# The first batch of a fused mixer and mixture-of-experts layer, rewritten as one instruction list per engine

## The chip, the cores and the metric

One core of a Trainium2 chip runs the whole program. The metric is the device time of one execution in microseconds, lower is better.

## The reference, cut to what matters

Sixteen batches of 512 tokens by 128 features go through one layer. First a state-space mixer with 8 heads of 64:

```python
z = x @ Wz; ssm = x @ Win              # ssm: B (64), C (64), dt (8), X (512)
delta = softplus(dt + dt_bias)
h = exp(-delta*exp(A_log)) * h + X_t (x) (delta*B_t);  y_t = h @ C_t     # scan over 512 tokens
y = y + D_param * X                    # the skip term
x = layernorm(x + (y * (silu(z) @ Wzg)) @ Wout)
```

Then a mixture of 12 experts of which 3 are chosen for each of three routers (`dw1`, `dw2`, `dw3`):

```python
h = gelu(sum_e (x @ W1[e].T) * dw1[:, e]);  y = sum_e (h @ W2[e].T) * dw2[:, e] + dw3 @ b2
x = layernorm(x + y)
```

## The kernel before, in words

Batches are numbered 0 to 15. Nearly all weights are held as a rounded part and a rest (`w_hi`, `w_lo`), and so are the operands they meet, so that one product is three matmuls (`mm3`, L223): hi by hi, hi by rest, rest by hi. W1 and W2 are 24 tiles of 128x512, tiles 0 to 11 W1, 12 to 23 W2. Each must be loaded, rounded (`w_hi`, ACT, L411) and its rest taken (`w_lo`, POOL, L415; the first two on DVE). `split_w` does that, `load_w` (L386, SP) the load into a slot that an earlier tile has left.

`program` (L1432) runs the same Python functions once for each engine; each function issues only what `eng` is. `mixer_alone` (L1275) does batch 0's mixer and routing and the front of batch 1's mixer. Then `body` (L1177) runs for b = 1 to 15: the experts of batch b-1 are interleaved with the heads of batch b's mixer. `mixture_alone` ends it.

The mixer of a batch: `mix_x` transposes x on PE; `mix_dt` and `mix_step` make delta, a chain of small POOL operations with one reciprocal on DVE (L527); `mix_bc`, `mix_z`, `mix_X`, `mix_zg` are products; `mix_rates` writes decays and their running products to DRAM, from where SP broadcasts one row for each head (`seg_row`, L684, into `seg_b`, and `start_row`, L688, into `ctd`); `mix_states` makes the chunk states. For each head, ACT scales the scores (`mix_score_step`, L782, `Gh`), DVE adds the skip term (`mix_score_skip`, L791) and scans the decays (`mix_decay`, L802), POOL multiplies the two (L809). For each pair of heads PE then runs `mix_y` (L827, L835) and DVE gates the result (L844); `mix_out` is the output product (L853). `seg_b` has two buffers: the row of head h+2 is loaded when scan h is over.

Routing: normalisation (`route_stats`, `route_scale`, L899), a transpose, logits (L943), `route_weights` on DVE (L963 to L987), and `route_rows`: the weights are transposed on PE (L1001), written to DRAM and read back as broadcast rows (`row_b`, L1017). An expert's input is that row times x (`expert_row`, DVE, L1032), rounded on ACT (L1053), its rest on POOL (L1056), then 12 matmuls (`expert_in`, L229 to L231).

What sets the order around the change is this one shared list of calls: every engine takes them in turn. `mix_bank` (L234) gives the mixer's products two PSUM banks in rotation; `keep_busy` (L1270) issues dummy matmuls. POOL takes the rests of tiles 2 to 15 before the first normalised rows are written:

```python
def first_weights_ready(eng):
    if eng in (PE, DVE, AC):
        eng.wait_ge(sems["w_lo0"], rests(N1 - 1))      # N1 = 16
```

since `x1` lies in a slot of the ring that the first 16 tiles pass through. The last two tiles are split among the first experts.

## Time and profile before

| what | value |
|---|---|
| median of 3 runs | 1603.38 us (1601.7 to 1604.11) |
| the profiled execution, its own time | 1602.08 us |
| its span, first to last instruction | 1600.0 us |
| mean granted TensorE clock | 0.993 |
| PE busy | 1564.8 us (98%) |
| first expert matmul of the program | 98.36 us after the span's start |

The span is what the trace covers; the execution's own time is 2.08 us longer. Starts in the trace count from the span's start.

### The profile page before, as it was taken

The page shows a single profiled execution, that of the slowest core. Times are in us where ns is not written, and L with a number is a line of the kernel's source. Part 1 is how long each engine was busy: PE and PEld are TensorE (multiplying, and loading weights), DVE is VectorE, ACT ScalarE, POOL GpSimd, SP SyncE. Part 2 cuts the span into 40 slices and gives each one's busy share as a digit, 9 for nine tenths or more (in the row PEclk, how much of TensorE's full clock was granted, in tenths as well). Part 3 has the DMA queues.
Part 4 walks back from the last instruction along what each step waited for, and adds up shares of the span by engine and source line. Part 5 has one row for each costly group of instructions (what it writes and reads, how often), then busy time and mean ns, then how long its engine had stood idle before and what let it go on. Part 6 is the DMA issues. An engine that isn't in the chain of part 4 may idle for free.

```text
span 1600.0 us, 25283 instructions
## 1 busy us (share of the span) xinstructions
PE 1564.8 (98%) x8632; PEld 1254.4 (78%) x8632; DVE 1105.2 (69%) x3105; ACT 593.8 (37%) x1356; POOL 655.0 (41%) x758
## 2 busy tenths in 40 slices
PE   7789999999999999999999999999999999999997
PEld 6667878787787877878788787878778787887876
DVE  6566677776767776687776767777676776757744
ACT  5542442524334252442425334242442415334130
POOL 5763351715436162351715435162351615335040
PEclk9899999999999999999999999999999999999999
DMA  4441230402214031230402214041230403213020
GB/s 143 136 127 40 64 97 28 133 14 86 76 42 117 28 112 42 65 96 28 133 14 91 77 42 118 22 117 36 64 96 28 133 14 100 68 49 112 21 66 7
DMA packets 81871, 115.30 MB, mean 72 GB/s; under 512 B 10176, under 2 KB 37328, under 8 KB 81744
## 3 DMA queue, kind: packets, MB, share of 16 engines
q1 hardware_dynamic: 81744, 113.71, 24.2%
q8 instruction: 68, 1.11, 0.3%
q14 instruction: 59, 0.48, 0.1%
HBM read 108.55 MB, written 5.13 MB: 71 GB/s over the span
## 4 chain that ended last, share of the span: by engine, by line
PE 94%; POOL 2%; DVE 1%; issue 1%; ACT 1%; DMA 1%; POOLq 0%; SPq 0%; DVEq 0%; ACTq 0%
PE exp_bank L229 23%; PE exp_bank L231 22%; PE exp_bank L230 22%; PE mix_bank L827 4%; PE mix_bank L229 4%; PE mix_bank L853 3%; PE mix_bank L231 3%; PE mix_bank L230 3%; PE mix_bank L835 3%; PE mix_bank L753 1%; PE turn_bank L1106 1%; PE mix_bank L701 1%; PE mix_bank L943 1%; PE mix_bank L502 1%; POOL w_lo L415 1%
## 5 line engine op out<-in xcount | busy, mean ns | idle before, releaser
L1056 POOL TENSOR_TENSOR sp_lo<-fbuf,sp_hi 128x512 fp32r<-128x512 f32 (+2 forms) x208 | 250.0, 1206 | 263.7 <-ACT sp_hi L1053 139.4
L229 PE MATMUL exp_bank<-w_hi,sp_hi 128*128 128x512 f32 x768 | 309.7, 403 | 2.0 <-POOL sp_lo L1099 2.0
L229 PE MATMUL exp_bank<-sp_hi,w_hi 128*128 128x512 f32 x768 | 307.8, 401 | 1.4 <-POOL sp_lo L1056 1.4
L231 PE MATMUL exp_bank<-w_hi,sp_lo 128*128 128x512 f32 x768 | 303.4, 395 | 0.0
L230 PE MATMUL exp_bank<-w_lo,sp_hi 128*128 128x512 f32 x768 | 303.1, 395 | 0.0
L231 PE MATMUL exp_bank<-sp_hi,w_lo 128*128 128x512 f32 x768 | 302.6, 394 | 0.0
L230 PE MATMUL exp_bank<-sp_lo,w_hi 128*128 128x512 f32 x768 | 301.1, 392 | 0.0
L1053 ACT CAST sp_hi<-fbuf 128x512 fp32r<-128x512 f32 (+2 forms) x208 | 122.0, 588 | 309.4 <-DVE fbuf L1032 266.6
L1145 DVE SCALAR_TENSOR_TENSOR acc<-exp_bank,dw,acc 128x128 f32<-128x128 f32 x384 | 132.3, 344 | 141.4 <-PE exp_bank L231 140.8
L229 PEld LDWEIGHTS exp_bank<-sp_hi,w_hi 128*128 128x128 f32 x768 | 144.1, 188 | 45.3 <-issue 13.7
L809 POOL TENSOR_TENSOR Wt<-Wt,Gh 128x512 f32<-128x512 f32 x128 | 176.3, 1378 | 6.2 <-DVE Wt L802 6.0
L535 POOL TENSOR_TENSOR delta<-delta,bias_b 128x32 f32<-128x32 f32 x16 | 4.0, 252 | 423.3 <-ACT delta L512 423.3
L229 PEld LDWEIGHTS exp_bank<-w_hi,sp_hi 128*128 128x128 f32 x768 | 144.3, 188 | 35.3 <-issue 2.0
L231 PEld LDWEIGHTS exp_bank<-w_hi,sp_lo 128*128 128x128 f32 x768 | 144.0, 188 | 35.1
L230 PEld LDWEIGHTS exp_bank<-w_lo,sp_hi 128*128 128x128 f32 x768 | 144.4, 188 | 31.6
L231 PEld LDWEIGHTS exp_bank<-sp_hi,w_lo 128*128 128x128 f32 x768 | 144.3, 188 | 30.9
L230 PEld LDWEIGHTS exp_bank<-sp_lo,w_hi 128*128 128x128 f32 x768 | 144.4, 188 | 30.0
L782 ACT ACTIVATE Gh<-Gm,delta 128x128 f32<-128x128 f32 x512 | 163.5, 390 | 9.8 <-POOL Wt L809 9.8
L802 DVE TENSOR_TENSOR_SCAN Wt<-seg_b,unit_bank 128x512 f32<-128x512 f32 x128 | 154.3, 1206 | 2.0 <-DMA seg_b<-dA_rows 2.0
L1032 DVE TENSOR_TENSOR fbuf<-turn_bank,row_b 128x512 f32<-128x512 f32 x192 | 129.5, 678 | 24.0 <-DMA row_b<-dw_rows 21.5
L1145 DVE SCALAR_TENSOR_TENSOR acc_odd<-exp_bank,dw,acc_odd 128x128 f32<-128x128 f32 x320 | 109.5, 342 | 0.0
L1099 POOL TENSOR_TENSOR sp_lo<-fbuf,sp_hi 128x512 fp32r<-128x512 f32 x32 | 42.6, 1330 | 134.4 <-DVE sp_hi L1093 134.4
(201 smaller groups left out, 2274.4 us busy)
## 6 DMA issues: line engine op xcount, KB each, us to landing
row_b<-dw_rows SPq DMA_DIRECT2D x192, 256.0 KB, 3.4
seg_b<-dA_rows SPq DMA_DIRECT2D x128, 256.0 KB, 3.6
ctd<-cum_rows SPq DMA_DIRECT2D x128, 96.0 KB, 3.3
x_in<-in_x SPq DMA_DIRECT2D x16, 256.0 KB, 2.8
result<-acc SPq DMA_DIRECT2D x16, 256.0 KB, 2.3
fbuf<-in_W1T SPq DMA_DIRECT2D x12, 256.0 KB, 3.1
fbuf<-in_W2T SPq DMA_DIRECT2D x4, 256.0 KB, 2.9
Gh<-in_W2T SPq DMA_DIRECT2D x4, 256.0 KB, 3.8
```

What stands on the lines that cost most here:

```text
L229: nc.tensor.matmul(ps, s_hi, m_hi, start=start and j == 0, stop=False)
L230: nc.tensor.matmul(ps, s_hi, m_lo, start=False, stop=False)
L231: last = nc.tensor.matmul(ps, s_lo, m_hi, start=False, stop=stop and j == n - 1)
L782: last = AC.activation(G[:, c, :], Gm[:, c, :], ACT.Copy, scale=delta[:, c, h:h + 1])
L802: sig("scan", DVE.tensor_tensor_scan(W, seg_b[h % 2][:, :], unit[:, :], 0.0, ALU.mult, ALU.add))
L809: sig("W", PO.tensor_tensor(W, W, Gh[h % 2][:, :, :].rearrange("p c t -> p (c t)"), ALU.mult))
L827: PE.matmul(ps[j * HD:(j + 1) * HD, tok(c)], Xd[:, c, h * HD:(h + 1) * HD], Wt[:, q % 2, at:at + P], start=(c == 0), stop=False)
L835: last = PE.matmul(ps[j * HD:(j + 1) * HD, tok(c)], S[n, c - 1, q * HD:(q + 1) * HD], ctd[n, q % 2, (c - 1) * P:c * P], start=False, stop= ...
L1032: sig("xw", DVE.tensor_tensor(wide[e % 2], rb[:, :], row_b[e % 2][:, :], ALU.mult))
L1053: sig("xw_hi", AC.copy(sp_hi[:, at, cols], wide[e % 2][:, cols]))
L1056: sig("xw_lo", PO.tensor_tensor(sp_lo[:, at, cols], wide[e % 2][:, cols], sp_hi[:, at, cols].bitcast(F32), ALU.subtract))
L1145: sig("comb", DVE.scalar_tensor_tensor(dst, ps, w, dst, ALU.mult, ALU.add))
```

## The change

The first batch, `mixer_alone`, is replaced by five lists, `start_pe` to `start_sp`, one for each engine, each with an order of its own. They lay out batch 0 and the front of batch 1 so:

- The products of the start get PSUM banks of their own (`START_BANK`: the experts' four banks and the turn bank).
- Batch 0's skip term is no longer added by DVE: POOL makes two tables of diagonals (`skip_tables`) and PE adds the term with 8 small matmuls for each pair of heads (`mix_y_skip`).
- Batch 0's decay rows have four buffers (`seg_b` twice, `acc`, `b2_sb`), so a row is loaded four heads ahead.
- The transpose, dt, BC, z and X products of batch 1 are placed between the heads of batch 0.
- `N1` falls from 16 to 12: only W1's tiles pass through the ring and are waited for ahead of `x1`. Tiles 12 to 15 are split in the routing, 16 to 23 during the first experts (`late_split`); tiles 2 and 3 have their rests taken by DVE.

From batch 2 on the program is as before. The diff, cut:

```diff
+START_BANK = {(0, f"zg{q}"): q for q in range(4)}
+START_BANK.update({(0, f"X{c}"): c for c in range(4)})
+START_BANK.update({(0, "z0"): 2, (0, "z1"): 3, (0, "lg"): 2, (0, "dwT"): 3, (1, "BC"): 0, (1, "dtB"): 1, (1, "z0"): 2, (1, "z1"): 3,
+                   (1, "X0"): 0, (1, "X1"): 1, (1, "xT"): 4})
+START_FREE = {(0, f"zg{q}"): ("Xd", 0, q + 1) for q in range(4)}
+START_FREE.update({(0, "X2"): ("silu", 0, 1), (0, "X3"): ("silu", 0, 2), (0, "lg"): ("silu", 1, 1), (0, "dwT"): ("silu", 1, 2), (1, "BC"): ("zg", 0, 1),
+                   (1, "dtB"): ("zg", 0, 2), (1, "z0"): ("zg", 0, 3), (1, "z1"): ("zg", 0, 4),
+                   (1, "X0"): ("BC", 1, 1), (1, "X1"): ("dt_raw", 1, 1)})
...
-        NW, RING, LATE = 2 * E, 4, 4
-        N1, NHP, LO_V = 16, 2, (0, 1)
-        late_slot = (0, 1, 2, 3, 0, 1, 4, 4)
+        NW, RING, LATE = 2 * E, 4, 6
+        N1, NHP, LO_V = 12, 2, (0, 1, 2, 3)
+        late_slot = (4, 2, 3, 0, 1, 5, 4, 5, 4, 5, 4, 4)
...
+        first_seg = [seg_b[0][:, :], seg_b[1][:, :], acc[:, :, :].rearrange("p c d -> p (c d)"),
+                     b2_sb[:, :, :].rearrange("p c d -> p (c d)")]
...
+                if first(b):
+                    DVE.wait_ge(sems[f"seg{h % 4}"], 16 * (h // 4 + 1))
+                else:
+                    wait(DVE, f"seg_in{h % 2}", b, h // 2 + 1)
                 wait(DVE, "ps_st", b)
                 if q >= 2:
                     wait(DVE, "ps_yq", b, q - 1)
-                sig("scan", DVE.tensor_tensor_scan(W, seg_b[h % 2][:, :], unit[:, :], 0.0, ALU.mult, ALU.add))
-            if eng is SP and h + 2 < H:
+                sig("scan", DVE.tensor_tensor_scan(W, first_seg[h % 4] if first(b) else seg_b[h % 2][:, :], unit[:, :], 0.0, ALU.mult, ALU.add))
+            ahead = 4 if first(b) else 2
+            if eng is SP and h + ahead < H:
                 wait(SP, "scan", b, h + 1)
-                seg_row(b, h + 2)
+                seg_row(b, h + ahead)
             if eng is PO:
                 wait(PO, "scan", b, h + 1)
-                wait(PO, "G_skip", b, h + 1)
+                wait(PO, "G_dt" if first(b) else "G_skip", b, h + 1)
                 sig("W", PO.tensor_tensor(W, W, Gh[h % 2][:, :, :].rearrange("p c t -> p (c t)"), ALU.mult))
...
+        def skip_tables(eng):
+            if eng is PO:
+                PO.wait_ge(sems["decay_par"], 48)
+                for n in range(2):
+                    PO.tensor_tensor(row_b[n][:, :].rearrange("p (h t) -> p h t", h=NC),
+                                     ident4[:, :].rearrange("p (h t) -> p h t", h=NC),
+                                     d_b[:, n * NC:(n + 1) * NC].unsqueeze(2).to_broadcast([P, NC, P]),
+                                     ALU.mult).then_inc(sems["diag"], 1)
+        def mix_y_skip(eng, b, q):
+            if eng is PE:
+                ps = mix_bank(b, f"y{q}")
+                PE.wait_ge(sems["diag"], 2)
+                wait(PE, "Xd", b)
+                for c in range(NC):
+                    for j in range(2):
+                        h = 2 * q + j
+                        PE.matmul(ps[j * HD:(j + 1) * HD, tok(c)], Xd[:, c, h * HD:(h + 1) * HD],
+                                  row_b[h // NC][:, tok(h % NC)], start=(c == 0), stop=False)
...
-                load_w(eng, [NW - 1])
+                split_w(eng, range(N1 + 4, N1 + 6))
                 if eng is AC:
-                    AC.wait_ge(sems["w_lo0"], rests(NW - 2))
...
+            late_split = ([18], [], [19], [20], [21], [22], [], [23])
+            late_load = ([], [19, 20], [], [21], [22], [], [23], [])
             for q in range(NQ):
                 mix_from_start(eng, b, q)
                 experts(eng, p, [e], ahead)
+                if not norm_before:
+                    split_w(eng, late_split[2 * q])
+                    load_w(eng, late_load[2 * q])
+                    if q == NQ - 1:
+                        if eng is SP:
+                            SP.wait_ge(sems["w_lo0"], rests(21))
+                        mix_load_next(eng, p)
                 mix_score_skip(eng, b, 2 * q + 1)
...
+        def start_pe(b, nxt):
...
+            mix_z(PE, b)
+            mix_X(PE, b, range(4))
+            PE.wait_ge(sems["masks"], 6)
+            PE.wait_ge(sems["cast"], 4)
+            mix_rates(PE, b)
+            mix_ends(PE, b)
+            router_product(PE)
+            keep_busy(rb, 6)
+            mix_scores(PE, b)
+            keep_busy(rb, 12)
+            mix_states(PE, b)
+            mix_x(PE, nxt, True)
+            PE.wait_ge(sems["router"], 1)
+            PE.wait_ge(sems["cast"], NCAST)
+            mix_zg(PE, b)
+            mix_y_skip(PE, b, 0)
+            mix_y(PE, b, 0)
+            mix_y_skip(PE, b, 1)
+            mix_dt(PE, nxt)
+            mix_y(PE, b, 1)
+            mix_bc(PE, nxt)
+            mix_y_skip(PE, b, 2)
+            mix_y(PE, b, 2)
+            mix_z(PE, nxt)
+            mix_y_skip(PE, b, 3)
+            mix_y(PE, b, 3)
+            keep_busy(rb, 6)
+            mix_out(PE, b)
+            mix_X(PE, nxt, range(2))
+            keep_busy(rb, 14)
+            route_transpose(PE, b)
+            route_logits(PE, b)
+            mix_scores(PE, nxt)
+            mix_rates(PE, nxt)
+            mix_ends(PE, nxt)
+            mix_X(PE, nxt, [2])
+            mix_zg(PE, nxt, range(2))
+            keep_busy(hb[3], 4)
+            route_rows(PE, b)
+            mix_zg(PE, nxt, range(2, 4))
+            mix_X(PE, nxt, [3])
+            keep_busy(hb[1], 6)
+            mix_states(PE, nxt)
+            keep_busy(hb[1], 10)
+            first_weights_ready(PE)
+        def start_dve(b, nxt):
...
+            split_w(DVE, range(0, 2))
+            mix_step(DVE, b)
+            mix_z(DVE, b)
+            mix_X(DVE, b, range(2))
+            mix_silu_split(DVE, b, on=DVE)
+            DVE.wait_ge(sems["zero"], 16)
+            mix_rates(DVE, b)
+            setup_zg(DVE)
+            mix_X(DVE, b, range(2, 4))
+            split_w(DVE, range(2, 4))
+            router_product(DVE)
+            mix_decay(DVE, b, 0)
+            mix_decay(DVE, b, 1)
+            mix_states(DVE, b)
+            mix_from_start(DVE, b, 0)
+            mix_x(DVE, nxt, True)
+            for q in range(1, NQ):
+                mix_decay(DVE, b, 2 * q)
+                mix_decay(DVE, b, 2 * q + 1)
+                mix_from_start(DVE, b, q)
+                mix_y(DVE, b, q - 1)
+            mix_step(DVE, nxt)
+            mix_y(DVE, b, NQ - 1)
+            mix_z(DVE, nxt)
+            mix_out(DVE, b)
+            route_stats(DVE, b)
+            first_weights_ready(DVE)
+            route_scale(DVE, b)
+            route_logits(DVE, b, on=DVE)
+            route_weights(DVE, b)
+            mix_rates(DVE, nxt)
+            expert_row(DVE, b, 0)
+            expert_row(DVE, b, 1)
+            mix_states(DVE, nxt)
+        def start_act(b, nxt):
...
+            mix_rates(AC, b)
+            mix_ends(AC, b)
+            mix_bc(AC, b)
+            split_w(AC, range(2, 6))
+            mix_scores(AC, b)
+            mix_score_step(AC, b, 0)
+            mix_score_step(AC, b, 1)
+            mix_x(AC, nxt, True)
+            mix_zg(AC, b, range(1))
+            mix_score_step(AC, b, 2)
+            mix_zg(AC, b, range(1, 3))
+            mix_score_step(AC, b, 3)
+            split_w(AC, [6])
+            mix_zg(AC, b, [3])
+            mix_score_step(AC, b, 4)
+            mix_score_step(AC, b, 5)
+            split_w(AC, [7])
+            mix_score_step(AC, b, 6)
+            split_w(AC, [8])
+            mix_score_step(AC, b, 7)
+            mix_dt(AC, nxt)
+            mix_bc(AC, nxt)
+            mix_step(AC, nxt, table=False)
+            split_w(AC, range(9, 12))
+            mix_z(AC, nxt)
+            AC.preload_act_table_set(LOG_EXP)
+            mix_silu_split(AC, nxt)
+            mix_X(AC, nxt, [0], on=AC)
+            route_stats(AC, b, table=False)
+            mix_X(AC, nxt, [1], on=AC)
+            first_weights_ready(AC)
+            split_w(AC, range(N1, N1 + 2))
+            route_transpose(AC, b)
+            mix_scores(AC, nxt)
+            mix_rates(AC, nxt)
+            mix_ends(AC, nxt)
+            mix_X(AC, nxt, [2], on=AC)
+            route_weights(AC, b)
+            mix_zg(AC, nxt, range(1))
+            route_rows(AC, b)
+            mix_zg(AC, nxt, range(1, 4))
+            mix_X(AC, nxt, [3], on=AC)
+            split_w(AC, range(N1 + 2, N1 + 4))
+            expert_split(AC, b, 0)
+            expert_split(AC, b, 1)
+        def start_pool(b, nxt):
+            neg_a_ready(PO)
+            mix_step(PO, b)
+            skip_tables(PO)
+            mix_ends(PO, b)
+            split_w(PO, range(4, 6))
             for q in range(NQ):
+                mix_decay(PO, b, 2 * q)
+                mix_decay(PO, b, 2 * q + 1)
+                if 0 < q < NQ - 1:
+                    split_w(PO, [5 + q])
+            mix_step(PO, nxt)
+            split_w(PO, range(8, 12))
+            load_b2(PO)
+            wait(PO, "x1", b)
+            mix_silu_split(PO, nxt)
+            wait(PO, "lg", b)
+            split_w(PO, range(N1, N1 + 2))
+            wait(PO, "dwr", b)
+            mix_ends(PO, nxt)
+            split_w(PO, range(N1 + 2, N1 + 4))
+            expert_split(PO, b, 0)
+            expert_split(PO, b, 1)
+        def start_sp(b, nxt):
+            load_w(SP, range(RING, RING + 2))
+            SP.wait_ge(sems["zero"], 16)
+            mix_rates(SP, b, start=False)
+            seg_row(b, 3)
+            start_rows(SP, b)
+            wait(SP, "ps_xT", nxt)
+            seg_row(b, 2)
+            load_w(SP, range(6, 8))
+            for h in range(2):
+                mix_decay(SP, b, h)
+            load_w(SP, [8])
+            mix_decay(SP, b, 2)
+            mix_y(SP, b, 0)
+            load_w(SP, [9])
+            mix_decay(SP, b, 3)
+            mix_y(SP, b, 1)
+            load_w(SP, range(10, 12))
+            wait(SP, "scan", b)
+            load_w(SP, range(N1, N1 + 3))
+            wait(SP, "W", b)
+            load_w(SP, range(N1 + 3, N1 + 5))
+            load_b2(SP)
+            wait(SP, "x1", b)
+            load_w(SP, [N1 + 5])
+            route_rows(SP, b)
+            expert_row(SP, b, 0)
+            expert_row(SP, b, 1)
+            load_w(SP, [N1 + LATE])
+            SP.wait_ge(sems["w_lo0"], rests(N1 + 2))
+            mix_rates(SP, nxt, start=False)
+            start_rows(SP, nxt)
```

How the lists move the work shows in three places. First DVE in batch 0's heads 2 to 5 (scan, skip, `ctd` product, gating). Before:

```order
L791 SCALAR_TENSOR_TENSOR Gh0<-unit_bank,d_b,Gh0 128x512 [waits G_dt]
L802 SCALAR_TENSOR_TENSOR Wt<-seg_b0,unit_bank 128x512 [waits seg_in0]
L791 SCALAR_TENSOR_TENSOR Gh1<-unit_bank,d_b,Gh1 128x512 [waits G_dt]
L802 SCALAR_TENSOR_TENSOR Wt<-seg_b1,unit_bank 128x512 [waits seg_in1]
L816 TENSOR_TENSOR ctd<-ctd,CT 128x384 [waits ctd_in1]
L844 TENSOR_TENSOR zg<-mix_bank0,zg 128x512 [waits zg,ps_yq]
L791 SCALAR_TENSOR_TENSOR Gh0<-unit_bank,d_b,Gh0 128x512 [waits G_dt]
L802 SCALAR_TENSOR_TENSOR Wt<-seg_b0,unit_bank 128x512 [waits seg_in0]
L791 SCALAR_TENSOR_TENSOR Gh1<-unit_bank,d_b,Gh1 128x512 [waits G_dt]
```

After:

```order
L831 TENSOR_TENSOR ctd<-ctd,CT 128x384 [waits BC,ctd_in0]
L497 TENSOR_TENSOR xT_lo<-xT,xT_hi 128x512 [waits xT]
L816 SCALAR_TENSOR_TENSOR Wt<-acc,unit_bank 128x512 [waits set_seg2]
L816 SCALAR_TENSOR_TENSOR Wt<-b2_sb,unit_bank 128x512 [waits set_seg3]
L831 TENSOR_TENSOR ctd<-ctd,CT 128x384 [waits ctd_in1]
L881 TENSOR_TENSOR zg<-mix_bank0,zg 128x512 [waits zg,ps_yq]
L816 SCALAR_TENSOR_TENSOR Wt<-seg_b0,unit_bank 128x512 [waits set_seg0]
L816 SCALAR_TENSOR_TENSOR Wt<-seg_b1,unit_bank 128x512 [waits set_seg1]
```

The skip additions into `Gh` are gone, each pair of scans stands together, and heads 2 and 3 read `acc` and `b2_sb`. Batch 1's `xT_lo` stands among them.

Second POOL from batch 1's front to the first heads of `body` (`w2_lo` is a tile's rest, `sp_lo` an expert's). Before:

```order
L731 TENSOR_TENSOR ends<-ends,delta 128x24 [waits ends]
L737 TENSOR_TENSOR Wt<-Xd,ends 128x512 [waits end_dt,silu_lo,Xd]
L737 TENSOR_TENSOR Wt<-Xd,ends 128x512 [waits Xd] x2
L1056 TENSOR_TENSOR sp_lo<-fbuf,sp_hi 128x384 [waits xw_hi]
L1056 TENSOR_TENSOR sp_lo<-fbuf,sp_hi 128x128 [waits xw_hi]
L1056 TENSOR_TENSOR sp_lo<-fbuf,sp_hi 128x512 [waits xw_hi]
L415 TENSOR_TENSOR w2_lo<-acc,w2_hi 128x512 [waits set_w_hi]
L1056 TENSOR_TENSOR sp_lo<-fbuf,sp_hi 128x512 [waits xw_hi] x3
L809 TENSOR_TENSOR Wt<-Wt,Gh0 128x512 [waits G_skip,scan]
L1056 TENSOR_TENSOR sp_lo<-fbuf,sp_hi 128x512 [waits xw_hi]
```

After:

```order
L426 TENSOR_TENSOR w2_lo<-seg_b1,w2_hi 128x512 [waits set_w_hi]
L426 TENSOR_TENSOR w2_lo<-Gh0,w2_hi 128x512 [waits set_w_hi]
L1094 TENSOR_TENSOR sp_lo<-fbuf,sp_hi 128x384 [waits xw_hi]
L1094 TENSOR_TENSOR sp_lo<-fbuf,sp_hi 128x128 [waits xw_hi]
L1094 TENSOR_TENSOR sp_lo<-fbuf,sp_hi 128x512 [waits xw_hi] x3
L426 TENSOR_TENSOR w2_lo<-Gh1,w2_hi 128x512 [waits set_w_hi]
L426 TENSOR_TENSOR w2_lo<-x_in,w2_hi 128x512 [waits set_w_hi]
L1094 TENSOR_TENSOR sp_lo<-fbuf,sp_hi 128x512 [waits xw_hi]
L824 TENSOR_TENSOR Wt<-Wt,Gh0 128x512 [waits G_skip,scan]
L1094 TENSOR_TENSOR sp_lo<-fbuf,sp_hi 128x512 [waits xw_hi]
L426 TENSOR_TENSOR w2_lo<-acc,w2_hi 128x512 [waits set_w_hi]
L824 TENSOR_TENSOR Wt<-Wt,Gh1 128x512 [waits G_skip,scan]
```

Where one rest stood among the experts' (and one more after the last head), eight now do, two of them ahead of expert 4. The three products of L745 (before L737) stand ahead of the piece after.

Third SP around the first expert's rows. Before:

```order
L1010 DMA dw_rows<-rows 48x128 [waits dwT]
L1017 DMA row_b0<-dw_rows 128x512 [waits dw_out]
L1017 DMA row_b1<-dw_rows 128x512
L668 DMA dA_rows<-dA_t 32x127 [waits set_w_lo0,dA]
L671 DMA cum_rows<-cum_t 32x128 [waits ecum,ctd]
L686 DMA seg_b0<-dA_rows 128x512 [waits rates_out]
L686 DMA seg_b1<-dA_rows 128x512
L1017 DMA row_b0<-dw_rows 128x512 [waits xw]
L1017 DMA row_b1<-dw_rows 128x512 [waits xw]
L692 DMA ctd<-cum_rows 64x384 [waits ps_yq]
L692 DMA ctd<-cum_rows 64x384 x3
L1017 DMA row_b0<-dw_rows 128x512 [waits xw]
```

After:

```order
L1048 DMA dw_rows<-rows 48x128 [waits dwT]
L1055 DMA row_b0<-dw_rows 128x512 [waits dw_out]
L1055 DMA row_b1<-dw_rows 128x512
L1055 DMA row_b0<-dw_rows 128x512 [waits xw]
L1055 DMA row_b1<-dw_rows 128x512 [waits xw]
L408 DMA acc<-in_W2T 128x512 [waits set_late4,set_w_lo0,set_w_hi]
L673 DMA dA_rows<-dA_t 32x127 [waits set_w_lo0,dA]
L676 DMA cum_rows<-cum_t 32x128 [waits ecum,ctd]
L694 DMA seg_b0<-dA_rows 128x512 [waits rates_out]
L694 DMA seg_b1<-dA_rows 128x512
L700 DMA ctd<-cum_rows 64x384 [waits ps_yq]
L700 DMA ctd<-cum_rows 64x384 x3
```

The rows of batch 1's decays (`dA_rows`, `cum_rows`, `seg_b`) stood ahead of the third and fourth expert rows; now they stand behind them, behind a tile's load, and behind the wait for tile 14's rest.

## Rows read from the trace of the kernel before

**Rows 1.** Windows: PE, PEld, DVE, ACT, POOL busy us (xinstructions), granted clock, DMA share, GB/s.

```profile
0.00:98.36 98.36, 74.74 (x489) 62.43 (x490) 57.34 (x134) 51.20 (x115) 60.73 (x91) 0.90 0.40 121
27.90:52.40 24.50, 21.97 (x196) 18.64 (x196) 20.50 (x26) 13.19 (x35) 18.34 (x14) 1.00 0.56 168
98.36:139.60 41.24, 41.24 (x257) 32.60 (x257) 27.81 (x37) 18.92 (x47) 27.47 (x21) 1.00 0.47 137
98.36:1600.00 1501.64, 1490.07 (x8143) 1191.93 (x8143) 1047.85 (x2972) 542.57 (x1242) 594.26 (x668) 1.00 0.24 69
```

**Rows 2.** Timeline, start of batch 0: start us, us, engine, what [idle before <-releaser].

```profile
10.70 0.25 POOL L535 TENSOR_TENSOR delta<-delta,bias_b 128x32 f32<-128x32 f32 x1 [5.92 <-ACT delta L512]
...
18.38 0.26 POOL L562 TENSOR_TENSOR a_lo<-a_rows,a_hi 128x32 fp32r<-128x32 f32 x1
...
8.70 0.16 DVE L457 TENSOR_SCALAR neg_a<-neg_a 128x8 f32<-128x8 f32 x1
...
15.20 0.35 DVE L527 RECIPROCAL dt_s<-dt_s 128x32 f32<-128x32 f32 x1 [2.60 <-POOL dt_s L547]
```

**Rows 3.** Timeline of ACT, DVE and PE, batch 0's heads and output product.

```profile
23.59 0.27 ACT L659 ACTIVATE dA_t<-mix_bank 32x128 f32<-32x128 f32 x1 [2.17 <-PE mix_bank L716]
...
31.07 2.33 DVE L802 TENSOR_TENSOR_SCAN Wt<-seg_b,unit_bank 128x512 f32<-128x512 f32 x2
...
48.65 0.75 DVE L791 SCALAR_TENSOR_TENSOR Gh<-unit_bank,d_b,Gh 128x512 f32<-128x512 f32 x1
...
52.95 1.09 PE L827 MATMUL mix_bank<-Wt,Xd 128*64 128x128 f32 x16 [0.73 <-POOL Wt L809]
...
55.64 3.84 PE L853 MATMUL mix_bank<-wout,zg 128*128 128x128 f32 x32 [0.80 <-DVE zg L844]
```

**Rows 4.** The chain of waits, in batch 0's heads: start us, us, what.

```profile
39.99 4.49 DMA seg_b<-dA_rows
```

**Rows 5.** Timeline of DVE, the normalised rows of batch 0.

```profile
63.31 0.16 DVE L893 TENSOR_TENSOR nrm<-nrm 128x4 f32<-128x4 f32 x1 [1.25 <-POOL w_lo L415]
...
64.10 2.06 DVE L899 TENSOR_SCALAR fbuf<-x_in,mv,nrm 128x128 f32<-128x128 f32 x4
```

**Rows 6.** Timeline of PE and DVE, the routing of batch 0 and, later, of batch 1.

```profile
70.97 1.85 PE L943 MATMUL exp_bank<-router,fbuf 128*128 128x36 f32 x8
...
77.60 0.96 DVE L963 MAX8 fbuf<-fbuf 128x8 f32<-128x12 f32 x12
...
84.88 1.03 DVE L976 TENSOR_TENSOR fbuf<-fbuf 128x144 f32<-128x144 f32 x1
...
87.98 0.23 DVE L987 TENSOR_TENSOR dwpad<-fbuf,srec 128x48 f32<-128x48 f32 x1
...
163.13 0.97 DVE L963 MAX8 fbuf<-fbuf 128x8 f32<-128x12 f32 x12
...
167.49 0.31 DVE L976 TENSOR_TENSOR fbuf<-fbuf 128x144 f32<-128x144 f32 x1
...
169.02 0.24 DVE L987 TENSOR_TENSOR dwpad<-fbuf,srec 128x48 f32<-128x48 f32 x1
```

**Rows 7.** The chain of waits, 88:100 us: one matmul at either clock.

```profile
90.09 0.43 PE mix_bank L229
...
98.84 0.23 PE exp_bank L230
```

**Rows 8.** Groups of POOL, 98.36:139.6 us: out<-in xcount | busy us, mean ns | idle before.

```profile
L1056 POOL TENSOR_TENSOR sp_lo<-fbuf,sp_hi 128x512 fp32r<-128x512 f32 x11 | 14.3, 1309 | 8.9 <-DVE Gh L791 7.4 <-ACT sp_hi L1053 1.5
L809 POOL TENSOR_TENSOR Wt<-Wt,Gh 128x512 f32<-128x512 f32 x8 | 11.0, 1376 | 0.0
L415 POOL TENSOR_TENSOR w_lo<-acc,w_hi 128x512 fp32r<-128x512 f32 x2 | 2.8, 1398 | 0.0
```

**Rows 9.** Timeline of DVE and SP: expert rows at the first experts.

```profile
105.14 0.69 DVE L1032 TENSOR_TENSOR fbuf<-turn_bank,row_b 128x512 f32<-128x512 f32 x1 [2.33 <-POOL sp_lo L1056]
...
101.90 1.31 SPq L1017 DMA_DIRECT2D row_b<-dw_rows  x2
```

328 lines of the change are left out of this document (119 added, 209 removed).

## The prediction

> **What bounds the kernel now.** I read the windows first. From the first expert on PE is busy 1490.07 us of 1501.64, at a granted clock of 1.00, and in the first stretch of experts 41.24 of 41.24 [rows 1]. Nothing but PE's own work sets the time there, and the change leaves that work alone. In the 98.36 us ahead of it PE is busy 74.74, dummy matmuls included, at a mean clock of 0.90 [rows 1]. That is the only place where something can be won: each microsecond by which the first expert starts earlier is one off the end, as long as PE then runs on without waits. So the question is when the first expert starts, and what waits the experts of batch 0 get.
>
> Then I follow batch 0 by its waits. Its dt chain begins on POOL at 10.70, when delta arrives, and ends at 18.64 [rows 2]. The decays' exponential is at 23.59, scan 0 at 31.07, the last pair's product at 52.95, the output product at 55.64 [rows 3]. Between them the path alternates between scans, products and the row for head h+2, fetched only when scan h has freed one of two buffers: 4.49 us from issue to use [rows 4]. Then POOL has tile rests on end, and DVE's normalisation goes on at 63.31, released by one of them [rows 5]. Routing begins at 77.60 and takes to 88.21 [rows 6]; the first expert is at 98.36.
>
> **The change part by part**, as starts in batch 0 now and then:
>
> 1. *dt chain.* dt comes ahead of BC on PE and ACT, so delta is no longer last. POOL waits for neg_a, written at 8.86, instead of starting at 10.70 [rows 2]: 1.8 less, end near 16.8. PE meets the transposition of the rates behind X2 and X3 alone (before, the scores and ten dummies stood there too). I put the exponential near 18, against 23.59 [rows 3]. From there to scan 0 were 7.5 us; ACT now has three BC copies and four tile casts ahead of the scores, so I keep nearly all of it: scan 0 near 25.1, **6.0 earlier**. Bounds: 1.8 (the dt gain alone) and 7.
>
> 2. *Heads.* DVE had eight skip additions of 0.75 [rows 3], 6.0 us; they go. PE gets four groups of eight small matmuls, each like the product's 1.09 at 52.95 [rows 3]: 4.4 us in its gaps, which are 23.6 us in all (98.36 less 74.74) [rows 1]. POOL makes the two tables, about 1.3 each, while it waits for `ends`. With four buffers the 4.49 us of a row [rows 4] lies under two scans and more. What is left is DVE's own list. From its first state operation to its third gating it was busy 20.50 us [rows 1], six skips of 0.75 among them: 16.0 without. Add batch 1's `xT_lo` (a 128x512 pass like a skip, 0.75), take off the gating behind the last scan (0.7), add POOL's last product (1.376) [rows 8]: 17.4. I give 1.6 to waits for rows and `ctd` halves that SP issues late: 19.0 instead of 21.9. The last pair's product is near 44.1, **8.9 earlier**.
>
> 3. *The reciprocal ahead of the last gating.* DVE's list has batch 1's reciprocal before the last gating. POOL begins that dt chain after its last head product, and the reciprocal came 4.5 us into the chain [rows 2]: 48.6. Gating follows at 49.0, though its product is ready at 46.0. The output product starts near 49.7, only 5.9 earlier. Here a wait is added, and mix_out is queued behind it.
>
> 4. *The gate of the normalised rows.* POOL: dt chain 7.9 us [rows 2], then tiles 8 to 11, rests of the form that took 1.309 [rows 8], 5.2: 57.2 against 63.31 [rows 5]. The normalisation itself, 49.7 plus 3.84 [rows 3] plus some 3.7 for sum, statistics and root, is at 57.2: POOL and DVE meet. **6.1 earlier**; the rows are written at 60.1 instead of 66.16.
>
> 5. *Routing.* Before, 11.4 us passed from the written rows (66.16) [rows 5] to the first maximum [rows 6], since batch 1's BC and dt products stood ahead of the logits and its tanh and gate ahead of the maxima. Those have moved between the heads. Left are the transposes and two copies (1.8) and the logits (1.85 even at the slow pace [rows 6]): 3.7. The maxima start near 63.8, 13.8 earlier. They took 10.6 us beside a busy POOL (77.60 to 88.21) and 6.1 in batch 1's routing beside an idle one (163.13 to 169.26) [rows 6]. Now POOL waits for `lg`, does two rests beside the maxima, then waits for the weights. I take the short figure: **18.3 earlier**.
>
> 6. *Up to the first expert* I keep 10.15 us (88.21 to 98.36): the same round trip through DRAM. The first expert starts near 80.1.
>
> 7. *The first experts.* POOL had 27.47 us of work in 41.24 [rows 1], two of them tile rests of 1.40 [rows 8]. It gets six more, 8.4 us: 35.9 in 41.2, 87%, in a fixed order. Expert 4 is the tight place. Its row was issued at 101.90, 3.5 after the first expert, and multiplied at 105.14 [rows 9]. Now SP has the decays' writes, their round trip and six row loads ahead of it, which I put at 5.8 after the first expert, multiplied at 9.2, its rest done at 11.9. PE is there after 4 x 12 matmuls of 0.23 [rows 7]: 11.0, so 0.9 late. From that rest's start, 10.6, to expert 11's are eight rests of 1.309, seven head products of 1.376 and five tiles of 1.398 [rows 8]: 27.1, so 37.7, where PE comes at 35.8 (eleven experts at 2.76, three pairs at 1.8). **1.9 us given back.** Bounds: 0 if DMA is prompt, 5 if POOL also idles between items as it did for 8.9 us beside DVE [rows 8]; a gain has no reason here, since PE had no wait.
>
> ACT's six more casts of about 0.6 lie under 41.24 us in which it was busy 18.92 [rows 1]; if POOL's tiles are late they queue behind it and cost what POOL costs. The late loads lie in slots that nobody else wants before batch 1's x is fetched.
>
> Sum: 18.3 less 1.9 is 16.4. Against the profiled execution's 1602.08 that is 1585.7. The median of the runs shown is 1.3 above it, 1603.38: **1587.0**.
>
> A rule weighed. DVE's L976, with both inputs in SBUF, took 1.03 us beside POOL's products and 0.31 beside an idle POOL [rows 6]. The Trainium skill, page SBUF — State Buffer, section Who interferes with whom, says that such a DVE instruction and a GpSimd one that reads SBUF lock each other out for a whole instruction; by that rule step 5's gain is real, and the trace agrees (1.03 against 0.31). The same rule speaks against step 7: the four `ctd` products among the experts would each wait for a product of a POOL that is hardly ever idle now, which by the rule alone is up to 5.5 us more of DVE's time (four times 1.376, an estimate).
>
> **Rivals.**
>
> *A, POOL holds the experts.* The lock just described, from the rows: four `ctd` products and each scan's hand-over wait up to one POOL instruction of 1.38 [rows 8]; DVE was busy 27.81 of 41.24 [rows 1], so much of it is hidden. If every one of the six added rests stops the expert behind it, 8.4 us go instead of 1.9: 9.9 gained, 1593.5. For it: the fixed order. Against: 5.3 us of POOL's time are left. 15%.
>
> *B, the start is held elsewhere.* One of the steps 1 to 4 keeps its old distance: PE at the slow pace (0.43 a matmul instead of 0.23 [rows 7]) has two zg products, 5.2 us instead of 2.8, ahead of the transposed weights; or tile 11's load, which waits for tile 7's rest, is late. Then some 11 us are gained: 1592.4. 17%.
>
> *C, slower than before.* PE now waits for POOL at expert after expert. After its wait for the routing weights PE ran at the lower of its two levels, 1.2 GHz: 0.43 a matmul at 90.09 instead of 0.23 [rows 7]. If the experts' stage of 41.24 us ran all at that level it would take some 41 more and the kernel 1626; it is slower than before once more than 44% of the stage (18.3 of 41.2) does. Against it: the stage had a clock of 1.00 [rows 1], and the waits that I count are under 2 us. 3%.
>
> *D, nothing moves.* The new lists start no sooner, or what the start wins is lost by PE waits later: within 0.2%, 1603. 3%.
>
> **How the numbers follow.** Forecast 62%, A 15%, B 17%, C 3%, D 3%. The time is the forecast's, 1587.0. Downwards the unknowns give 1 us in step 1 (its bound of 7), 1.9 in step 7, 1.6 in step 2 and 2.5 where POOL's dt chain or the DRAM trip is prompt: 1580. Upwards A is at 1593.5; with a part of step 1's bound the range goes to **1594.5**. Of C, D and the tails under 2 in 10 are left out. A measurement of this kernel can tell about 0.2%, 3.2 us. Faster 94%, same 3%, slower 3%.
>
> **What would show it.** First expert at 78 to 82 us; scan 0 near 25, the last pair near 44, output product near 50 with DVE released by its reciprocal; a short route (about 6 us); POOL above 85% busy over the first 41 us of experts and PE waits for it of 1 to 3 us there; from batch 1's outputs on, PE as before. Wrong would be a first expert after 85, a clock under 0.95 in that stage, or waits above 5 us.

## The result, and the profile after

The changed kernel takes **1587.15 us** (median of 4 runs, 1585.12 to 1589.09) against 1603.71 us before on the same chip: a ratio of 0.9899, with a 95% interval of 0.9882 to 0.9916. The same kernel again on another chip gave 1586.68 us (5 runs, 1584.6 to 1591.16), ratio 0.9906, 0.9891 to 0.9922.

The profiled execution is the slowest of the first four: 1589.09 us, span 1587.0. That matters below, so the second profile, called the control, stands beside it where the two differ (its own 1586.68 us, span 1584.5). The profile of the kernel before was 1.6 us faster than the median measured beside the changed kernel, and this one is 1.9 us slower than its own: so the two profiles differ by 13.0 us where the medians differ by 16.6.

The windows of the changed kernel, with the columns of [rows 1]:

```profile
0.00:79.99 79.99, 67.86 (x523) 57.15 (x524) 49.03 (x129) 48.50 (x109) 54.74 (x85) 0.98 0.43 129
79.99:121.23 41.24, 38.74 (x218) 30.53 (x219) 27.82 (x36) 20.63 (x51) 34.07 (x27) 0.96 0.60 175
79.99:1587.00 1507.01, 1492.91 (x8143) 1193.12 (x8143) 1048.32 (x2971) 546.32 (x1248) 601.49 (x674) 1.00 0.24 70
```

The start ends at 79.99 us instead of 98.36, 18.37 us earlier, but the program ends only 13.0 us earlier. The second line shows where a part went: PE is busy 38.74 of the 41.24 us in which it was busy throughout before, at a mean clock of 0.96.

The timeline of the changed kernel, places that answer to [rows 2, 3, 5, 6]:

```profile
8.95 0.29 POOL L539 TENSOR_TENSOR delta<-delta,bias_b 128x32 f32<-128x32 f32 x1 [4.63 <-DVE neg_a L459]
...
16.92 0.53 POOL L567 TENSOR_TENSOR a_lo<-a_rows,a_hi 128x32 fp32r<-128x32 f32 x1
...
25.72 1.52 PE L761 MATMUL mix_bank<-Wt,B_tok 128*64 128x256 f32 x12
...
27.36 2.33 DVE L816 TENSOR_TENSOR_SCAN Wt<-seg_b,unit_bank 128x512 f32<-128x512 f32 x2 [3.05 <-PE mix_bank L761]
...
46.79 1.09 PE L864 MATMUL mix_bank<-Wt,Xd 128*64 128x128 f32 x16 [0.54 <-POOL Wt L824]
...
50.30 0.35 DVE L530 RECIPROCAL dt_s<-dt_s 128x32 f32<-128x32 f32 x1 [4.09 <-POOL dt_s L552]
...
51.25 3.84 PE L890 MATMUL mix_bank<-wout,zg 128*128 128x128 f32 x32 [1.03 <-DVE zg L881]
...
58.84 0.17 DVE L931 TENSOR_TENSOR nrm<-nrm 128x4 f32<-128x4 f32 x1 [1.25 <-POOL w_lo L426]
...
59.64 1.11 DVE L937 TENSOR_SCALAR fbuf<-x_in,mv,nrm 128x128 f32<-128x128 f32 x4
...
63.74 0.96 DVE L1001 MAX8 fbuf<-fbuf 128x8 f32<-128x12 f32 x12
...
66.97 0.74 DVE L1010 TENSOR_TENSOR fbuf<-iota_e,ix 128x144 f32<-128x144 f32 x3
68.09 0.31 DVE L1014 TENSOR_TENSOR fbuf<-fbuf 128x144 f32<-128x144 f32 x1
69.62 0.24 DVE L1025 TENSOR_TENSOR dwpad<-fbuf,srec 128x48 f32<-128x48 f32 x1
```

Read down it: scan 0 (L816) is 3.7 us earlier than in [rows 3], the last pair's product 6.2, the output product 4.4, the normalised rows 4.5 (start of L937, against 64.10 in [rows 5]), the maxima 13.9, the last weight 18.4. The route itself, 63.74 to 69.86, takes 6.12 us where it took 10.6.

Next PE's waits in the first experts (engine, line and what it waited for: us in all, times, longest; the shorter of the two, 0.9 us, stands ahead of the first expert), the windows around the longest, and SP's queue (SPq) and DVE and POOL behind it:

```profile
PE exp_bank L238 <- POOL sp_lo L1094: 3.4, 2, 2.5
```

```profile
92.00:94.00 2.00, 0.27 (x1) 0.27 (x2) 2.00 (x3) 1.51 (x5) 1.59 (x2) 1.00 0.45 102
94.00:96.00 2.00, 2.00 (x8) 1.52 (x8) 2.00 (x4) 1.27 (x3) 1.82 (x2) 0.73 0.46 163
96.00:98.00 2.00, 2.00 (x6) 1.57 (x5) 1.98 (x4) 1.67 (x5) 2.00 (x3) 0.50 0.48 164
98.00:100.00 2.00, 2.00 (x9) 1.64 (x8) 2.00 (x3) 0.78 (x3) 2.00 (x2) 0.92 0.88 220
```

```profile
79.74 0.31 SPq L676 DMA_DIRECT2D cum_rows<-cum_t  x1
83.38 0.81 SPq L694 DMA_DIRECT2D seg_b<-dA_rows  x2
84.29 2.40 SPq L700 DMA_DIRECT2D ctd<-cum_rows  x4
86.79 5.28 SPq L1055 DMA_DIRECT2D row_b<-dw_rows  x3
...
90.99 0.69 DVE L1070 TENSOR_TENSOR fbuf<-turn_bank,row_b 128x512 f32<-128x512 f32 x1 [7.92 <-DMA row_b<-dw_rows]
...
92.41 1.27 POOL L1094 TENSOR_TENSOR sp_lo<-fbuf,sp_hi 128x512 fp32r<-128x512 f32 x1 [4.20 <-DVE Gh L799]
```

PE names POOL, but POOL itself had been idle for 4.20 us and DVE for 7.92: the row of expert 4 was issued only at 86.79, because SP waited from 79.74 to 83.38 for the decays' stores and then issued six loads. PE stood for 2.5 us, and behind it the granted clock was 0.73 and then 0.50 (the 1.2 GHz level) over some 4 us. Of the 4.4 us lost (below) 2.5 are this wait; most of the other 1.9 goes with the low clock, since the control, at a clock of 1.00, loses only 0.7 beyond its wait.

To account for the 13.0 us I take the same operation in both kernels, DVE's sum of x and the output product in batch 2 (the third of its 16; rows of one tile: line, operation, count, duration, start):

```profile
L857 DVE TENSOR_TENSOR x_in<-mix_bank,x_in x1: 692/692/692, 242.1 to 242.1; 128x512 f32<-128x512 f32 x1
```

```profile
L895 DVE TENSOR_TENSOR x_in<-mix_bank,x_in x1: 691/691/691, 228.1 to 228.1; 128x512 f32<-128x512 f32 x1
```

The first is of the kernel before, the second of the changed one. From the first expert to this point before took 242.1 - 98.36 = 143.7 us, and now 228.1 - 79.99 = 148.1. So 18.4 earlier, less 4.4 at the first experts, is 14.0; the last 1.0 is lost somewhere in the 13 batches from there to the same operation of batch 15 (1244.7 us before and 1245.7 now). The control has 146.4 and 1245.2: 18.66 - 2.7 - 0.5, which is 15.5.

### The profile page after: what moved, and what is told of

It is laid out like the page before. It is cut to its first block, busy times and chain, and to the rows that moved or that the text cites. A ratio compares the mean times of both kernels' runs of the same rounds, so it can differ in the third digit from the quotient of the medians.

```text
span 1587.0 us, 25350 instructions
## 1 busy us (share of the span) xinstructions
PE 1560.8 (98%) x8666; PEld 1250.3 (79%) x8666; DVE 1097.4 (69%) x3099; ACT 594.8 (37%) x1357; POOL 656.2 (41%) x758
## 4 chain that ended last, share of the span: by engine, by line
PE 93%; POOL 3%; issue 1%; DVE 1%; DMA 1%; ACT 0%; SPq 0%; POOLq 0%; DVEq 0%; ACTq 0%
PE exp_bank L238 23%; PE exp_bank L240 22%; PE exp_bank L239 22%; PE mix_bank L864 4%; PE mix_bank L890 3%; PE mix_bank L238 3%; PE mix_bank L240 3%; PE mix_bank L239 3%; PE mix_bank L872 3%; PE mix_bank L761 1%; PE turn_bank L1144 1%; PE mix_bank L709 1%; PE mix_bank L981 1%; PE mix_bank L505 1%; POOL Wt L824 1%
## 5 line engine op out<-in xcount | busy, mean ns | idle before, releaser
L816 DVE TENSOR_TENSOR_SCAN Wt<-seg_b,unit_bank 128x512 f32<-128x512 f32 x124 | 149.5, 1207 | 3.0 <-PE mix_bank L761 3.0
```

The lines of the kernel that those rows point to most:

```text
L816: sig("scan", DVE.tensor_tensor_scan(W, first_seg[h % 4] if first(b) else seg_b[h % 2][:, :], unit[:, :], 0.0, ALU.mult, ALU.add))
```

## The experiments

Eleven runs follow, each against the kernel before, one of them of the changed kernel itself. The table gives the ratio to it, the marks that the readings below use, and "first stretch", the time from the first expert to batch 2's sum (143.7 before). Times in us. Medians of runs on different chips are better compared by their ratios, whose intervals reach some 2.4 us to either side; the marks are of one profiled execution each.

| kernel | median | ratio (95%) | scan 0 | rows (L937) | first expert | first stretch |
|---|---|---|---|---|---|---|
| changed | 1587.15 | 0.9899 (0.9882 to 0.9916) | 27.36 | 59.64 | 79.99 | 148.1 |
| control, the same | 1586.68 | 0.9906 (0.9891 to 0.9922) | 27.34 | 59.62 | 79.70 | 146.4 |
| rows 4, 5 first | 1585.32 | 0.9890 (0.9874 to 0.9905) | 28.55 | 60.84 | 81.51 | 143.7 |
| gate first | 1586.77 | 0.9902 (0.9886 to 0.9917) | 27.24 | 58.84 | 80.14 | 145.9 |
| skips on DVE | 1586.97 | 0.9903 (0.9889 to 0.9916) | 26.24 | 60.96 | 81.22 | 145.3 |
| two row buffers | 1589.11 | 0.9915 (0.9901 to 0.9928) | 26.24 | 61.82 | 83.68 | 145.0 |
| few fillers | 1584.00 | 0.9885 (0.9870 to 0.9900) | 27.33 | 58.90 | 79.15 | 145.2 |
| POOL beside | 1588.28 | 0.9912 (0.9897 to 0.9927) | 27.79 | 60.08 | 82.55 | 146.1 |
| best | 1580.85 | 0.9865 (0.9850 to 0.9880) | 26.57 | 57.59 | 77.40 | 143.7 |
| best, more moved | 1582.50 | 0.9871 (0.9854 to 0.9887) | 27.40 | 58.70 | 79.08 | 143.7 |
| best, skips on DVE | 1584.42 | 0.9884 (0.9868 to 0.9901) | 26.32 | 60.23 | 80.49 | 143.7 |
| best, no fillers | 1582.07 | 0.9872 (0.9856 to 0.9889) | 26.33 | 56.76 | 76.57 | 145.3 |

My theory after the result: the last 2 to 4 us are lost at expert 4 by SP's order. The rival: they are lost by POOL, or by the bandwidth of the transfers.

**Rows 4 and 5 first.** In `mix_rates`, for batch 1, and both rows taken out of `body`'s list for SP:

```diff
+                if b.reg is None and b.off == 1:
+                    expert_row(SP, b.prev(), 2)
+                    expert_row(SP, b.prev(), 3)
                 wait(SP, "rates_out", b)
```

> Only the queue of SyncE is changed: the rows of experts 4 and 5 are issued between the store of the cumulated decays and the wait for it, no longer behind that wait, two decay rows and four state rows. Theory 1 (order of the queue): the changed kernel loses 2.5 us before expert 4, because that row is issued at 86.79 us, and about 1.7 us more in the 4 us behind it, in which TensorE's granted clock is at the lower level. The row is now issued near 83 us, lands near 86 to 87 us, TensorE waits for nothing between 81 and 96 us and its clock stays at 1.00: about 4 us less than the changed kernel, near 1583.0 us. Theory 2 (bandwidth): the rows share the DMA engines with the W2 tile and the decays' store, the DMA share is 0.90 there already, the row lands no earlier than 89 us or the decay rows of the next batch come late in its place: 0 to 1.5 us less, 1585.6 to 1587 us.

Measured: the row is issued at 84.03 and multiplied 5.9 us after the first expert instead of 11.0; the first 41.24 us of experts have PE busy throughout at a clock of 1.00, and the first stretch is 143.7 us again, as before. First the timeline of SP and DVE, then the windows of the first 16 and the first 41.24 us of experts:

```profile
84.03 0.94 SPq L1058 DMA_DIRECT2D row_b<-dw_rows  x2
...
87.39 0.69 DVE L1073 TENSOR_TENSOR fbuf<-turn_bank,row_b 128x512 f32<-128x512 f32 x1 [2.84 <-DMA row_b<-dw_rows]
```

```profile
81.51:97.51 16.00, 16.00 (x70) 13.15 (x71) 11.22 (x16) 8.33 (x21) 13.00 (x11) 1.00 0.68 195
81.51:122.75 41.24, 41.24 (x257) 32.76 (x258) 28.16 (x37) 22.54 (x53) 35.20 (x27) 1.00 0.58 174
```

Theory 1 holds for the mechanism: POOL is busy 13.00 of the 16 us and 35.20 of the 41.24, with the same added tiles ahead of it, and PE never waits for it. For the size it does not hold: 1583.0 was expected and 1585.32 measured, under 2 us below the changed kernel, with intervals that overlap. This profile's start is 1.5 us later (scan 0 at 28.55), though no edit stands ahead of it, and the other profiles with the old order mostly lose less than the first one; that these two make up the difference in the medians is not shown.

**The control.** No edit.

> The changed kernel as it is, once more, on the chip of the three runs beside it. Its earlier profile fell on the slowest of four executions. If the time before expert 4 is a race between transfers that comes out differently each time, this profile has a wait there other than 2.5 us (1.6 us stood in the profile of the kernel that gates first); if scan 0 is set by TensorE's clock at the filler products, it does not start at 27.36 us again, but between 26.2 and 28.6 us, as in the four profiles so far. Median 1587 us, within 1 us.

Measured: scan 0 at 27.34, within 0.02 of the first profile, but a longest wait of 2.0 us and no fall of the clock behind it, 2.7 us lost instead of 4.4. The row comes in a race that ends a little differently each time: over the seven profiles with SP's old order the longest wait in the first 16 us of experts was 2.5, 2.0, 1.6, 0.7, 0.7, 0.8 and 1.8 us, in the order of the table.

**Gate first.** In `start_dve` the last gating goes ahead of the reciprocal:

```diff
-            mix_step(DVE, nxt)
             mix_y(DVE, b, NQ - 1)
+            mix_step(DVE, nxt)
```

> VectorE gates the last pair of batch 0 before it takes the reciprocal of the next batch's step chain, as the kernel before did in effect. The product of the last pair is done at 48.68 us and the reciprocal can't start before 50.30 us, so the gating fits in the gap at no cost. Theory 1 (GpSimd's W2 gate binds): the output product starts 1.8 us earlier, near 49.4 us, but the wait for GpSimd's tiles 8 to 11 grows from 1.25 to about 3 us and the normalised rows are written at the same 60.8 us: first expert at 80.0 us, 1587 us, within 1 us of the changed kernel. Theory 2 (VectorE's own chain binds, the gate is only what the profile names): everything behind moves 1.3 to 1.8 us: 1585.4 us.

Measured: the gating is at 48.20, the sum at 53.30 (1.8 earlier), and DVE then waits 2.46 us for POOL instead of 1.25. The rows are written 0.8 us earlier, but not through the edit: POOL began its chain 0.8 us earlier (45.91 instead of 46.70), since the waits for `ctd` rows in the heads happened to be shorter. The edit itself gave nothing at the rows, and the 0.8 did not reach the maxima either, which start at 63.81, where they were. The windows show why:

```profile
56.00:60.00 4.00, 1.78 (x16) 1.59 (x15) 1.77 (x8) 1.67 (x4) 2.48 (x3) 1.00 0.00 0
60.00:64.00 4.00, 3.31 (x16) 3.05 (x17) 0.50 (x4) 0.59 (x1) 2.71 (x3) 0.56 0.26 69
```

PE ran out of fillers, stood 2.2 us, and did the transposes and logits mostly at 1.2 GHz. Theory 1 (1586.77 us), with a second absorber that I had not named.

**Skips on DVE.** The skip term of batch 0 as before, in the changed kernel:

```diff
+            mix_score_skip(DVE, b, 0)
             mix_decay(DVE, b, 0)
...
-            mix_y_skip(PE, b, 0)
-            skip_tables(PO)
```

> The skip term of batch 0 goes back to VectorE: eight operations of 0.74 us between the scans, no skip tables on GpSimd (2.03 us for two), no extra products on TensorE; all else as in the changed kernel. Theory 1 (the heads go by VectorE): the heads take 5.9 us more, less the 1.0 us that VectorE waits in them and up to 1.6 us that the missing tables give scan 0: 3.3 to 5 us later everywhere, if nothing behind absorbs it 1590.5 to 1592 us. Theory 2 (the heads go by GpSimd's products, or the gate behind them absorbs it): less than 1 us, 1587 to 1588 us.

Measured: no difference in the median. From scan 0 to the reciprocal it took 25.4 us instead of 22.9, so the skips cost 2.5 in the heads. Scan 0 was 1.1 earlier, which is not the missing tables' doing: with the tables in place it is at 26.24 too (two row buffers), and both profiles have a granted clock of 1.00 in 18 to 26 us where the control has 0.79. The first expert is 1.5 later than in the control, and 1.1 of that came back at expert 4, whose row was multiplied at 90.39, as in the control (90.20). So one part of the 2.5 us is hidden by the clock of this profile and another absorbed at expert 4; the same edit on the best kernel, below, has neither.

**Two row buffers.**

```diff
-            ahead = 4 if first(b) else 2
+            ahead = 2
```

> Batch 0 has its decay rows in two buffers again, each issued when the scan two heads earlier is over; all else as in the changed kernel. Theory 1: a row takes 2.5 to 4.5 us from issue to use, while two heads later comes 2.3 to 3.7 us behind; VectorE waits about 1 to 2 us twice: 1588.5 to 1591 us. Theory 2 (with the state work, the decays and the gatings between the scans two buffers are enough): within 1 us of the changed kernel, 1587 us.

Measured: 1589.11, three waits for rows where the changed kernel has none, the longest

```profile
41.44 1.22 DVE L816 TENSOR_TENSOR_SCAN Wt<-seg_b,unit_bank 128x512 f32<-128x512 f32 x1 [2.94 <-DMA seg_b<-dA_rows]
```

and 0.95 and 1.21 beside it: 5.1 us in all. From scan 0 to the reciprocal it took 26.2 us instead of 22.9, so 3.3. The first expert is 4.0 later than in the control: 1.1 less from scan 0, and 1.8 more behind the rows, where PE ran at a clock of 0.59 and 0.56 (64 to 72 us) and had the transposed weights late; whether that hangs on the edit is not shown. The median is 2.4 later than the control's, 1.4 by the ratios, whose intervals overlap. Theory 1 by the rows.

**Few fillers.**

```diff
-            keep_busy(rb, 12)
+            keep_busy(rb, 3)
             mix_states(PE, b)
```

> Between the scores G and the states of batch 0 TensorE runs 3 filler products in place of 12. Theory 1 (TensorE's own queue sets scan 0): the fillers took 3.1 us, from 22.69 to 25.8 us, and the states began at 25.72 us though their last input was written at 25.11 us; with 3 they wait for that input alone: scan 0 near 26.3 to 26.8 us, 0.6 to 1 us earlier, and up to 2 us where the clock was low; median 0.5 to 1.5 us less, near 1586 us. Theory 2 (the fillers hold the clock): without them the states and the gate products behind run at 1.2 GHz, the states take 3 us in place of 1.5, scan 0 comes at the same time or up to 1.5 us later: 1587 to 1588.5 us.

Measured: 1584.0. In this profile PE was at the low level earlier, and the scores ended 1.8 us later than in the changed kernel (22.83 plus 1.91 against 20.82 plus 2.08); yet the states began at the same time:

```profile
22.83 1.91 PE L709 MATMUL mix_bank<-CT,BT 128*128 128x128 f32 x8
24.54 1.23 PE L1320 MATMUL turn_bank<-ident 128*128 128x128 f32 x6
25.70 1.52 PE L761 MATMUL mix_bank<-Wt,B_tok 128*64 128x256 f32 x12
```

The states took 1.52 in both, so the fillers taken away did not hold the clock. But scan 0 is at 27.33, where the control has it and not near 26.3 to 26.8, and the 0.55 us by which the first expert is earlier arose in the heads, where the control's wait of 0.73 us for a `ctd` row is missing: this profile alone decides nothing. A pair of others does. "Rows 4, 5 first" and "best" agree up to here (the scores at 22.15 in both, a granted clock of 0.60 and 0.59 in 18 to 26 us, POOL's last input at 25.7) but for the 12 and the 3 fillers:

```profile
26.92 1.51 PE L764 MATMUL mix_bank<-Wt,B_tok 128*64 128x256 f32 x12
28.55 2.33 DVE L819 TENSOR_TENSOR_SCAN Wt<-seg_b,unit_bank 128x512 f32<-128x512 f32 x2 [3.66 <-PE mix_bank L764]
```

```profile
24.94 1.51 PE L764 MATMUL mix_bank<-Wt,B_tok 128*64 128x256 f32 x12
26.57 2.33 DVE L819 TENSOR_TENSOR_SCAN Wt<-seg_b,unit_bank 128x512 f32<-128x512 f32 x2 [1.71 <-PE mix_bank L764]
```

That is 2.0 us for the 9 fillers where the clock is low. Where it is high they cost nothing: scan 0 is at 26.24 with 12 (two row buffers, clock 1.00) and at 26.33 with 3 (best, no fillers, 0.99), where the states waited for POOL. Theory 1, as far as the clock lets it. The median is 2.7 us below the control's on the same chip, with intervals that just overlap; some 1 us of it has no row.

**POOL beside the route.** The wait for the routing weights ahead of batch 1's `mix_ends` is taken from POOL:

```diff
-            wait(PO, "dwr", b)
             mix_ends(PO, nxt)
```

> GpSimd no longer waits for the routing weights before it forms the decayed inputs of batch 1: its 3.3 us of work run beside the second half of VectorE's routing. Theory 1 (a VectorE operation with both inputs in SBUF slows down beside a GpSimd one; the changed kernel's route of 6.1 us rests on that wait): the route takes 8.5 to 9.5 us again, its equality operations 0.6 to 1.0 us in place of 0.25 us, and all behind is 2.5 to 3.5 us later: 1589.5 to 1590.5 us. Theory 2 (the route was shorter for other reasons, such as its place): route 6.1 us, 1587 us, or a little less since the decayed inputs are ready earlier.

Measured: POOL's decayed inputs run from 67.08 to 70.4, and under them the three equality operations:

```profile
67.08 3.34 POOL L745 TENSOR_TENSOR Wt<-Xd,ends 128x512 f32<-128x512 f32 x3 [0.20 <-POOL ends L739]
...
67.41 3.17 DVE L1010 TENSOR_TENSOR fbuf<-iota_e,ix 128x144 f32<-128x144 f32 x3
70.62 0.31 DVE L1013 TENSOR_TENSOR fbuf<-fbuf 128x144 f32<-128x144 f32 x1
```

3.17 us instead of 0.74, and at 70.62, with POOL idle, 0.31 again. The route takes 8.6 us instead of 6.1, the first expert is 2.9 later than in the control (0.45 of it from scan 0). The median is 1.6 later, short of the 1589.5 that was expected and within the control's spread. Theory 1 by the rows; its price in the median is not told by these runs.

**Best.** Rows 4 and 5 first, few fillers, gate first, and

```diff
-        N1, NHP, LO_V = 12, 2, (0, 1, 2, 3)
+        N1, NHP, LO_V = 12, 2, (0, 1, 2, 3, 8)
...
-            keep_busy(rb, 14)
+            keep_busy(rb, 19)
             route_transpose(PE, b)
...
-            split_w(PO, range(8, 12))
+            split_w(PO, range(9, 12))
...
+            split_w(DVE, [8])
             mix_y(DVE, b, NQ - 1)
```

> The rows of experts 4 and 5 ahead of the wait in SyncE's queue, 3 fillers before the states, the last pair gated before the reciprocal, the low part of W2-gate tile 8 on VectorE in the gap before that gating in place of GpSimd, and 19 fillers in place of 14 before the transposes, so that TensorE's clock holds until the rows come. If the parts add: 2 to 4 us at expert 4, 0.6 to 1 at scan 0, 1.9 before the transposes, since GpSimd ends its three tiles 1.3 us earlier and starts 0.8 us earlier: 4.5 to 6.5 us less than the changed kernel, 1581 to 1582.5 us. If the gate only changes its owner, or the clock falls before the transposes as it did in the kernel that gates first (granted clock 0.66 in 60 to 70 us): 1583 to 1585 us.

Measured: 1580.85, ratio 0.9865 (0.9850 to 0.9880), 6 us below the changed kernel and with an interval apart from both of its intervals. 4.5 to 6.5 were expected, so the parts add. Against the control the profile gains 0.8 at scan 0, 2.0 at the rows, 2.3 at the first expert, 2.7 more in the first stretch. In DVE's timeline POOL still releases the norm, but at 56.79; PE's wait for the rows is 0.6 us, and the window of the first 16 us of experts is without a wait:

```profile
56.79 0.16 DVE L934 TENSOR_TENSOR nrm<-nrm 128x4 f32<-128x4 f32 x1 [1.25 <-POOL w_lo L426]
```

```profile
77.40:93.40 16.00, 16.00 (x70) 13.15 (x71) 11.22 (x15) 8.37 (x21) 12.98 (x11) 1.00 0.65 195
```

**Best, more moved.** Against the best kernel:

```diff
-            skip_tables(PO)
             mix_ends(PO, b)
+            skip_tables(PO)
...
+            split_w(DVE, [9])
             mix_z(DVE, nxt)
...
-            keep_busy(rb, 6)
+            keep_busy(rb, 3)
             mix_out(PE, b)
```

> The best kernel so far, with four more edits: GpSimd forms the decayed inputs of batch 0 before the skip tables; the low part of tile 9 too is VectorE's, in the gap behind the reciprocal; 3 fillers in place of 6 before the output product, and 17 in place of 19 before the transposes. If each reading holds: the tables (2.0 us) no longer stand before the decayed inputs, which then wait for their own input copies, so scan 0 comes 1.0 to 1.6 us earlier, near 25.3 us; the output product starts at 48.16 us instead of 48.80 us in the terms of the earlier run; GpSimd ends its W2-gate tiles 1.25 us earlier, about when VectorE's own statistics are done: together 2.2 to 2.9 us less, 1578 to 1578.7 us. If another wait takes the place (tables late for the first pair's product, the last row's transfer in the heads, a low clock at the transposes): 1579.5 to 1581 us.

Measured: 1582.5, no gain, and above both ranges. The first reading was wrong: POOL's first step waited 2.7 us for ACT's exponentials (`total`), not for the tables, took 1.32 us, and the decayed inputs began at 21.96 (21.70 in the best kernel). In the best kernel the exponentials were there at 19.56 and the tables done at 20.0, so 0.4 us was all that the swap could give; here the exponentials came 0.8 later, behind products at a clock of 0.54, and scan 0 at 27.40. Tile 9 moved the gate from POOL to ACT's root (0.61 us), with DVE's own small operation at 56.22 taking 1.08 us beside POOL's tiles instead of 0.32.

**Best, skips on DVE.** The skip edit on the best kernel.

> The best kernel so far with the skip term of batch 0 on VectorE again. In the changed kernel the same edit moved the last gating by 1.3 us and the median by nothing that can be told. Theory 1 (there it was absorbed at expert 4, whose row came at its own time): with expert 4's row no longer late, the full 1.3 us show, 1581.5 to 1583 us. Theory 2 (it is absorbed before the first expert, at GpSimd's W2 gate): the rows are written at the same time as in the best kernel, 1580.5 to 1581 us.

Measured: 1584.42, 3.6 us above the best by the medians and 3.0 by the ratios, the first expert 3.1 later. The first stretch is 143.7 in both, so nothing is absorbed at expert 4, and scan 0 moved by only 0.25: theory 1, and more than it said. From scan 0 to the reciprocal 25.8 instead of 22.9 is 2.9 us; PE waits 3.6 us for POOL's product of a head and goes on at 1.2 GHz, 1.98 us for a product of 1.09 (the changed kernel with the skips on DVE has the same, after 3.4 us):

```profile
38.58 1.98 PE L867 MATMUL mix_bank<-Wt,Xd 128*64 128x128 f32 x16 [3.64 <-POOL Wt L827]
```

**Best, no fillers.**

```diff
-            keep_busy(hb[1], 6)
             mix_states(PE, nxt)
-            keep_busy(hb[1], 10)
             first_weights_ready(PE)
```

> The best kernel so far without the 16 fillers around the states of batch 1, so that TensorE has nothing to do before the first expert but those states. Theory 1 (what TensorE did just before sets the clock it starts with): the granted clock is near 0.5 in the first 3 to 4 us of the first expert, its products take 0.5 us in place of 0.23 each, 1.5 to 2.5 us more in all, and then it rises and stays: 1582 to 1583.5 us. Theory 2 (the rival of the prediction in which the clock stays low): much of the stage from 78 to 100 us at the lower level, 1590 us or more. Theory 3 (fillers are for nothing): 1580.8 us as before.

Measured: 1582.07, 1.2 above the best (1.1 by the ratios, whose intervals overlap); PE waits 4.0 us and starts the experts at the lower level,

```profile
76.00:80.00 4.00, 3.43 (x9) 2.77 (x10) 3.42 (x6) 0.97 (x2) 1.93 (x3) 0.57 0.51 171
80.00:84.00 4.00, 4.00 (x19) 3.25 (x18) 0.69 (x1) 1.73 (x5) 4.00 (x4) 1.00 0.85 237
```

and the first stretch is 1.6 longer; the clock then stays. By the rows theory 1. The fall of the clock that rival C of the prediction feared is there, but it ends after some 4 us and does not last for the stage of 41 us.

## Why the prediction was right, and where it was not

The time, 1587.0, was measured at 1587.15 and 1586.68, and the first expert, forecast near 80.1, is at 79.99 and 79.70. Some of this is luck: scan 0 was 2.3 us later than forecast, and that error shrank to 1.6 us at the output product, 0.7 at the written rows and nothing at the maxima, since three later terms had been taken too long: the reciprocal, the four row operations and the logits. At the other end more was given back at expert 4 than forecast (4.4 and 2.7 us for 1.9), and 1.0 and 0.5 us more in the later batches, for which there was no term. By the profiles 13.0 and 15.5 us were gained where 16.4 were forecast; that the median fits to a few tenths owes something to the spread of the runs.

1. *dt chain: mis-sized.* It begins at 8.95 and ends at 17.45, 0.6 late since four of POOL's small operations took 0.53 to 0.71 us instead of some 0.25, with DVE at work beside it. The exponential came at 18.38, as forecast. But scan 0 came 3.7 us earlier and not 6.0. "I keep nearly all of it" was the step: 9.0 us passed from the exponential to scan 0 where 7.1 were kept. POOL's three decayed inputs took 3.97 us beside DVE (3.04 before), and the 3.1 us of fillers stood ahead of the states. The pair of profiles with 12 and 3 fillers shows the second, no run the first; the bounds, 1.8 to 7, held it.
2. *Heads: right in the sum, not in the parts.* From scan 0 to the last product were 19.4 us, 19.0 forecast. The rows in four buffers are worth 3.3 there (two row buffers), the skips 2.5 to 2.9, not their 6.0 of DVE time: put back, they partly filled time that DVE had lost otherwise, such as the 1.0 us wait for a `ctd` row at 40.66 and the 1.43 us of the operation behind it (0.53 with the skips).
3. *Reciprocal ahead of the gating: right.* The product was done at 48.68, and DVE gated at 50.57, released by its reciprocal. That came 3.6 us into the chain, where I had taken 4.5, so the output product started at 51.25 (49.7 forecast) and not 0.9 later still. The run that gates first starts it at 49.52, and gains nothing by it.
4. *Gate: right.* POOL's tiles ended at 58.81 and released DVE; the rows were written at 60.75 (60.1). DVE's own side would have been there at 57.6: close to the meeting that I had forecast, with POOL 1.2 us behind. The four row operations took 1.11 us, not the 2.06 that I had kept from [rows 5].
5. *Routing: right.* 6.12 us for 6.1, maxima at 63.74 for 63.8 (the logits took 1.08 us, where I had kept the 1.85 of the slow pace). The rule that I weighed is what decides the 6.12: with POOL beside it, the same list took 8.6. By the Trainium skill (SBUF — State Buffer, section Who interferes with whom) a DVE instruction with two SBUF inputs contends with a GpSimd one that reads SBUF, for ports that only one of them holds at a time; the trace agrees, 3.17 us against POOL's 3.34 in the same stretch. The larger part of this step is the other one: 3.0 us from the written rows to the maxima instead of 11.4, since batch 1's products stand between the heads. The rows of the two kernels show it, 8.4 of the 18.4 us; no run takes it back by itself, nor dt ahead of BC, nor N1 of 12.
6. *Up to the first expert: right*, 10.1 us.
7. *First experts: right place, wrong size, wrong part of the cause.* Expert 4 was named, and SP's order too; 1.9 us given back were forecast, 4.4 and 2.7 measured. The term that was mis-sized is the row's multiplication, put 9.2 us after the first expert: it was 11.0 and 10.5. In the first profile 1.0 us of the 1.8 is the issue, at 6.8 instead of 5.8 (the decays' round trip took 3.6 us, the issues of the `ctd` loads 2.4), and 0.8 the row itself, 4.2 us from issue to use where I took 3.4. What was lost beyond the wait, 1.9 us with the low clock and 0.7 in the control, was in no term. My second line, POOL's 27.1 us of ordered work up to expert 11, cost nothing: with the row early, PE did not wait once in 41.24 us, with POOL busy 35.20 of them. So rival A, POOL holding the experts, is refuted.

Of the signs named, the waits (2.5 and 2.0 us) and the first expert are as forecast, POOL's share just under (34.07 of 41.24 us, 83%), and the clock of that stage, 0.96, just above the 0.95 that was to mean wrong. Rival B would have had the first expert at 87 or later; rival C's fall of the clock did occur, for some 4 us after the longest wait.

## What to carry to other kernels

When a start is shortened, look for the transfers that keep their own timetable: a part of a saving upstream is then absorbed behind them, and the queue's order is the edit that releases it. Measure a part's worth in the version where nothing absorbs it, and look at the marks ahead of the edit too: by the medians the skip edit was worth nothing in the changed kernel and some 3 us in the best one, but in the first case only 1.1 us was absorbed, and as much was an earlier scan 0 that the edit had not caused. Where PE names a waiter, follow back through its idle time to the first engine that was not idle; it was SP here, two engines behind.

## What was not expected of the hardware

- Filler products have a length as well as a use. Twelve records took between 1.60 and 2.93 us in different profiles of the same list, and scan 0 lay between 26.24 and 28.55 us over the twelve profiles behind edits that mostly came later. In the start of this kernel the granted clock of 18 to 26 us was anything from 0.54 to 1.00; what decides it these runs do not show.
- DVE's twelve maxima took 0.96 us with POOL at work on tile rests and 0.97 beside an idle POOL [rows 6], while three elementwise operations with two inputs in SBUF took 3.17 us beside POOL and 0.74 without it. The Trainium skill (SBUF — State Buffer, section Who interferes with whom) has this too: a DVE instruction with at most one SBUF input, outside its two-port modes, does not contend. So work for POOL belongs under the maxima, as the changed kernel has it.
- After the wait of 2.5 us PE ran at 1.2 GHz for some 4 us, after the one of 2.0 us in the control it ran on at 2.4; the whole loss was 4.4 us in the first case and 2.7 in the second. The length of a wait alone does not tell: ahead of the transposes and the logits PE waited 1.2 and 0.7 us both in the control and with the skips on DVE, and from 64 to 68 us the clock was 1.00 in the one and 0.58 in the other.
